# Audio tower on one core: the middle stage rebuilt around four filter buffers, quarter stores and a split triangular solve

## The chip, the cores and the metric

The kernel runs on one core of a Trainium2 chip. The metric is the device time of one execution in microseconds (us), lower is better. Everything is 32-bit float. The engines are named as the profile names them: PE (TensorE, matrix products), PEld (its weight loads), DVE (VectorE), ACT (ScalarE), POOL (GpSimd) and SP (SyncE, which only issues transfers here).

## The reference, cut to what matters

The input is `x`, 32 batches of 750 tokens by 256 features. Tokens are padded to 768, cut into segments of 256 and every second one is kept, so 384 tokens per batch remain, in three blocks of 128.

1. `h = softmax(x x^T / 16) x` inside each block.
2. `h += attn(layernorm(h))`: q, k and v projections with a causal convolution of 4 taps and SiLU; a delta rule in chunks (of 32 in the reference, 128 in the kernel); a short (3 taps) and a long (63 taps) causal filter over v; a gate of two layers over the features and the means and deviations of the four branches; a softmax over the branches; a mixture, a norm and the output projection.
3. `h += ffn(layernorm(h))`: a router picks 2 of 6 experts; each expert is 256 -> 128 -> 256 with GELU.

The delta rule needs, for each chunk, the inverse of `I + A` with `A` strictly lower triangular:

```python
A = jnp.tril(jnp.einsum('bhnid,bhnjd->bhnij', kbc, kc), -1)
T = jnp.linalg.inv(jnp.eye(chunk, dtype=q.dtype) + A)
fir_long = causal_dwconv(vf, fir_long_w.reshape(NH * DV, FIR_L))   # 63 taps per channel
```

## The kernel before, in words

Each engine runs a queue of its own, written out by hand in program order; they meet only through semaphores. A `Signal` is a semaphore with so many increments per iteration; `now(it)` waits for this iteration's, `before(it, back)` for an earlier one's. There are three stages, separated by blocks: no engine enters the next block until all have left the one before.

**First stage** (`first_phase`): block attention, projections, convolutions, the products for `A`. It writes per batch the packs `packa` (q, k, v and scales), `packb` (residual, normed input, short filter) and the 32 x 32 `systems` (1,536 of them: 32 batches x 12 head-blocks x 4) to DRAM, keeps v of all batches in `v_all` (128 partitions x 256 channels x 96 columns), and expands the filter taps to the matrices `toeplitz` in DRAM.

**Middle stage** (`second_phase`), which the change rebuilds:

- PE (L909, L913) runs 32 iterations of 8 channels. Each has two halves of 4 channels; a half is 4 products of a 128 x 128 filter matrix with 96 columns of `v_all` and 4 of a 128 x 62 one with 64 columns. The profile counts each product as two matmuls, so 8 of each per half. The matrices come through two buffers `toep` that SP loads (L896), 760 KB per iteration.
- ACT (L926) copies each half out of PSUM into `stage`, 384 columns. After half of the channels it stores them to DRAM as `fl` in three pieces of 2 MB, one before each further part of its loop; the other half of the channels is written over the part of `v_all` that was read, and stored in three pieces after the last copy (L931). ACT leaves the block when all six have landed.
- DVE inverts the systems by columns: 12 per partition in four groups of three, each group a memset of the diagonal (L965) and 30 columns of two operations, a product (L970) and a sum (L974). POOL loads a group (L951) and stores it when solved (L954). Group g holds every partition's systems 3g to 3g+2, which are a quarter of the systems of every batch.

Then come, one after another with all engines in step: `prime`, a block in which SP increments the third stage's signals; and a block in which SP loads that stage's weights (L832), the first packs (L1111, L1117), the filtered values (L1114), the residual (L1120) and the solved systems into `UF` (L1108), while ACT and DVE compute a few constants and DVE clears `UF`, `TL`, `S`, `SGT` and part of `w1s` (L1142 to L1175). SP loads `UF` only after DVE's clears.

**Third stage** (`third_phase`): a software pipeline of bodies, one per batch, in which batch n is in the delta rule, `it = n-1` in the gate and the mixture, `e = n-2` in the router and the first experts, and `f = n-3` in the last experts. On DVE a body is, in this order: masks of the products (`mask`, L1653), `branch_statistics`, `transpose_diagonal` (L1659), `add_expert(f, 3)`, `residual(e)`, `add_expert(f, 4)`, `input_stats(n)` (L1664; it waits for the loads of pb and fl), `second_norm(e)` (L1775), `gate_logits(it)` (L1711, waits for PE's L1361), `add_expert(f, 5)`, `gate_weights`, `weigh`, `state(n, 0)` (L1685), the router, and the remaining additions (L1740, L1826). On PE the gate's products (L1350, L1354, L1361) stand between the merges of the inverse (L1254 to L1284, which read `UF` and `TL`) and `updates(n, 0)` (L1313). SP's body stores the result, loads the next packs each after the wait for its buffer's last reader, and then `load_u(n + 2)`. DVE writes out the first four bodies and loops over the others two by two.

Of the kernel before, what the change touches and what calls it, by code (L numbers as in the profile page):

```python
# [10 lines left out]
P = 128  # L11
D = 256
# [15 lines left out]

QT, KBT, KT, KTOK, VTOK = (n * HALF * T for n in range(5))
# [22 lines left out]

def even_heads_first(blk, h):

    return (h % 2) * (NM // 2) + blk * (NH // 2) + h // 2


def audio_tower(nc, x, w, out):
    NB = x.shape[0]
    NSYS = NB * NM * NQ // P  # L60
    with ExitStack() as ctx:
# [8 lines left out]
        def signal(name, per=1, primed=1):  # L70
# [7 lines left out]
            "fl": nc.dram_tensor("fl", [NB, P, BLK * D], F32, kind="Internal").ap(),  # L78
# [12 lines left out]
        shared = dict(expanded=expanded, NB=NB, NSYS=NSYS, dram=dram, bank=bank, ident=ident, upper=upper)  # L91
        make_constants(nc, ctx, ident, upper)
        with nc.sbuf_tensor("v_all", [P, D, BLK * NB], F32) as v_all:
            first_phase(nc, x, w, shared, v_all)
            second_phase(nc, shared, v_all)
        third_phase(nc, w, out, shared, third_phase_weights(nc, ctx))


# [709 lines left out]
def third_phase_weights(nc, ctx):  # L808
    def sb(name, shape):
# [15 lines left out]
    loaded = ctx.enter_context(nc.semaphore("p3_weights"))  # L825
    return dict(w1g=w1g, w1s=w1s, b1g=b1g, w2g=w2g, b2g=b2g, wo=wo, onw=onw, router=router, anchors=anchors,
                rclip=rclip, w1e=w1e, w2e=w2e, itemp=itemp, loaded=loaded)


def load_third_phase_weights(nc, sp, w, tail):  # L830
    def load(dst, src):
        sp.dma_start(dst, src).then_inc(tail["loaded"], 16)  # L832

    load(tail["w1g"][:, :, :], w["mlp_w1"][0:D].rearrange("(a p) n -> p a n", a=HALF))
    load(tail["w1s"][0:GATE_S, :], w["mlp_w1"][D:])
    load(tail["w2g"][:, :, :], w["mlp_w2"].rearrange("(m p) n -> p m n", m=MC))
    load(tail["wo"][:, :, :], w["Wo"].rearrange("(a p) n -> p a n", a=HALF))
    for e in range(NE):
        load(tail["w1e"][:, :, e, :], w["ffn_w1"][e].rearrange("(a p) n -> p a n", a=HALF))
    load(tail["w2e"][:, :, :], w["ffn_w2"].rearrange("e p n -> p e n"))  # L840
    load(tail["b2g"][:, :], w["mlp_b2"].partition_broadcast(P))
    load(tail["anchors"][:, :, :].rearrange("p e d -> p (e d)"), w["ffn_anchors"].rearrange("e d -> (e d)").partition_broadcast(P))
    load(tail["rclip"][:, :], w["ffn_routing_temp"].partition_broadcast(P))
    load(tail["itemp"][:, :], w["gate_log_temp"].partition_broadcast(P))
    for half in range(2):
        load(tail["onw"][half * DH:(half + 1) * DH, :], w["o_norm_w"].unsqueeze(1))
    with nc.allow_non_contiguous_dma(reason="a few columns, once"):
        load(tail["b1g"][:, :], w["mlp_b1"].rearrange("(m p) -> p m", m=MC))
        for a in range(HALF):
            load(tail["router"][:, a, :], w["ffn_proj_w"][:, a * P:(a + 1) * P].rearrange("e p -> p e"))  # L850


def second_phase(nc, shared, v_all):


    NB, NSYS, dram, bank, expanded = (shared[k] for k in ("NB", "NSYS", "dram", "bank", "expanded"))
    CG = 8
    SG = 3
    with ExitStack() as c:
# [9 lines left out]
        toep = [sb(f"toep{s}", [P, CG, TW]) for s in range(2)]  # L869
        Xs = [sb(f"X{s}", [P, SG, SC, SC]) for s in range(2)]  # L870
        GC = D // 2
        GI = GC // CG

        stage = [sb("stage", [P, BLK * NB, GC]),
# [13 lines left out]
        with nc.Block() as block:  # L888
# [30 lines left out]
            def _(act):  # L919
# [16 lines left out]
                for b in range(BLK):  # L936
                    store(0, b)
                    copy_pairs(1, b * 2, b * 2 + 2 if b < BLK - 1 else GI // 2)
                act.wait_ge(*fl_copied.now(2 * GI - 1))
                for b in range(BLK):  # L940
                    store(1, b)
# [1032 lines left out]
```

## Time and profile before

| | us |
|---|---|
| median of 3 runs (2932.5 to 2945.92) | 2935.69 |
| the profiled execution, its own time | 2936.39 |
| its span in the trace | 2934.7 |
| PE busy in the span | 2552.5 (87%) |
| DVE busy in the span | 1916.4 (65%) |
| ACT busy in the span | 1371.2 (47%) |
| POOL busy in the span | 532.7 (18%) |
| mean granted TensorE clock, share of full speed | 0.888 |

The profile cuts the span into 40 equal slices of 73.4 us and gives the busy tenths of each engine in each. `PEclk` is the granted TensorE clock in tenths of full speed; 0.50 is 1.2 GHz and 1.00 is 2.4 GHz. The first stage ends in the 11th slice, the middle stage fills slices 11 to 14. Elsewhere, rows have a start, a duration, the engine, the line of the kernel, the operation with its output and input, shapes and count, and in square brackets how long the engine had been idle and who ended that.

### The profile page before, as it was taken

What the parts mean: (1) busy time and instruction counts of PE and PEld (TensorE: products, weight loads), DVE (VectorE), ACT (ScalarE), POOL (GpSimd) and SP (SyncE); (2) the same over time, 40 slices, a digit from 0 to 9 for tenths busy, and PEclk for the clock granted to TensorE, in tenths of its full rate; (3) what the DMA queues carried; (4) which work ended last, traced back from release to release, by engine and by line L of the source; (5) the groups of instructions that cost most, each with busy time, mean ns of one, the idle gap of its engine ahead of it and who ended that gap; (6) DMA issues with size and microseconds to landing.
All of it is one profiled execution on the core that took longest, in us unless ns stands there. A gap on an engine that the chain in (4) does not pass through costs nothing.

```text
span 2934.7 us, 60213 instructions
## 1 busy us (share of the span) xinstructions
PE 2552.5 (87%) x21024; PEld 1936.5 (66%) x21024; DVE 1916.4 (65%) x5240; ACT 1371.2 (47%) x2626; POOL 532.7 (18%) x375
## 2 busy tenths in 40 slices
PE   5888888888699279999999999999999999999997
PEld 3666666666588257767676766766766677667765
DVE  4888898888599024655665765566566647655664
ACT  3777777777222123443444434434534444344442
POOL 1333333333100001111111111111111111111110
PEclk9999999999655557998999999999999999999998
DMA  2566566666567612212211311221122113111200
GB/s 73 197 215 205 190 214 202 200 205 207 194 213 235 192 68 95 66 58 87 81 63 58 108 59 64 66 100 65 58 91 77 63 58 107 60 64 63 101 17 16
DMA packets 233222, 334.12 MB, mean 114 GB/s; under 512 B 113696, under 2 KB 198656, under 8 KB 223776
## 3 DMA queue, kind: packets, MB, share of 16 engines
q1 hardware_dynamic: 207168, 305.89, 31.6%
q10 hardware_dynamic: 24672, 12.58, 1.5%
q0 software_dynamic: 1152, 12.58, 1.1%
q8 instruction: 144, 2.36, 0.3%
q14 instruction: 86, 0.70, 0.1%
HBM read 191.68 MB, written 164.23 MB: 121 GB/s over the span
## 4 chain that ended last, share of the span: by engine, by line
PE 42%; DVE 11%; ACT 6%; issue 6%; DVEq 0%; ACTq 0%; POOL 0%
PE bank L1407 6%; PE bank L1417 6%; PE bank L1350 5%; PE bank L1361 3%; PE bank L1379 3%; PE bank L1245 3%; PE bank L1328 3%; ACT L1554 3%; PE bank L1354 2%; PE bank L1313 2%; PE bank L1276 2%; PE bank L1284 2%; DVE DL L1740 1%; DVE HA L1826 1%; DVE bst L1762 1%
## 5 line engine op out<-in xcount | busy, mean ns | idle before, releaser
L1407 PE MATMUL bank<-YT,w1e 128*128 128x384 f32 x768 | 321.1, 545 | 1.2 <-ACT HE L1554 1.2
L683 DVE SCALAR_TENSOR_TENSOR Y<-bank,convw,Y 128x383 f32<-128x383 f32 (+2 forms) x576 | 315.2, 607 | 6.0 <-ACT Y L559 6.0
L1417 PE MATMUL bank<-w2e,HE 128*128 128x256 f32 x1152 | 308.9, 407 | 10.8 <-DVE HA L1826 7.8
L1826 DVE SCALAR_TENSOR_TENSOR HA<-bank,we,HA 128x256 f32<-128x256 f32 x576 | 242.8, 476 | 112.5 <-PE bank L1417 108.7
L411 PE MATMUL bank<-pb,wqkv 128*128 128x384 f32 x768 | 286.4, 503 | 10.4 <-DVE pb L667 9.5
L1711 DVE TENSOR_TENSOR L<-bank,b2g 128x48 f32<-128x48 f32 x32 | 6.6, 208 | 420.2 <-PE bank L1361 420.2
L1417 PEld LDWEIGHTS bank<-w2e,HE 128*128 128x128 f32 x1152 | 219.0, 201 | 51.6 <-issue 14.7
L1554 ACT ACTIVATE HE<-bank 128x384 f32<-128x384 f32 x192 | 94.3, 491 | 232.7 <-PE bank L1407 232.0
L1350 PE MATMUL bank<-qb,w1g 128*128 128x384 f32 x512 | 201.8, 517 | 0.4 <-ACT GH L1546 0.4
L1407 PEld LDWEIGHTS bank<-YT,w1e 128*128 128x128 f32 x768 | 150.5, 214 | 75.5 <-issue 27.8
L1245 PE MATMUL bank<-qa 64*128 64x256 f32 x768 | 118.9, 431 | 92.2 <-PEq L1123 57.9
L1537 ACT ACTIVATE ATM<-bank 128x192 f32<-128x192 f32 x192 | 60.2, 331 | 296.0 <-DVE ATM L1653 296.0
L411 PEld LDWEIGHTS bank<-pb,wqkv 128*128 128x128 f32 x768 | 138.4, 197 | 84.3 <-issue 14.7
L783 POOL TENSOR_TENSOR RR<-RS,minus_half 128x24 f32<-128x24 f32 x32 | 133.3, 4166 | 272.0 <-DVE RS L732 272.0
L1929 POOL TENSOR_TENSOR ta<-qb,WT 128x768 f32<-128x768 f32 x32 | 72.6, 2267 | 542.7 <-DVE WT L1730 542.7
L1245 PEld LDWEIGHTS bank<-qa 64*128 64x128 f32 x768 | 71.5, 199 | 139.6 <-issue 125.9
L559 ACT ACTIVATE Y<-bank,convw 128x384 f32<-128x384 f32 x192 | 112.2, 584 | 79.9 <-PE bank L411 78.8
L909 PE MATMUL bank<-v_all,toep 128*128 x512 | 129.5, 434 | 20.6 <-DMA toep<-toeplitz 17.5
L1935 POOL TENSOR_TENSOR m<-m,minus_half_q 128x12 f32<-128x12 f32 x32 | 72.6, 2270 | 372.9 <-DVE m L1746 372.9
L909 PEld LDWEIGHTS bank<-v_all,toep 128*128 128x128 f32 x512 | 114.0, 328 | 28.3 <-issue 21.6
L1328 PEld LDWEIGHTS bank<-W,ATM 128*128 128x128 f32 x768 | 108.0, 212 | 35.8 <-ACT W L1529 25.7
L1328 PE MATMUL bank<-W,ATM 128*128 128x64 f32 x768 | 114.5, 298 | 15.0 <-ACT W L1529 15.0
(220 smaller groups left out, 5459.2 us busy)
## 6 DMA issues: line engine op xcount, KB each, us to landing
packa<-pa SPq DMA_DIRECT2D x32, 1932.0 KB, 6.3
qa<-packa SPq DMA_DIRECT2D x32, 1932.0 KB, 7.7
packb<-pb SPq DMA_DIRECT2D x32, 768.0 KB, 5.1
qb<-packb SPq DMA_DIRECT2D x32, 768.0 KB, 6.7
toeplitz<-taps SPq DMA_DIRECT2D x128, 190.0 KB, 4.4
toep<-toeplitz SPq DMA_DIRECT2D x32, 760.0 KB, 4.2
packb<-fsk SPq DMA_DIRECT2D x32, 384.0 KB, 2.3
fl<-fl SPq DMA_DIRECT2D x32, 384.0 KB, 5.4
```

What stands on the lines that cost most here:

```text
L411: mm = pe.matmul(proj_bank[j][:, 0:T], wqkv[:, a, j * P:(j + 1) * P], xnT[:, a, :], start=(a == 0), stop=(a == HALF - 1))
L559: act.activation(Y[:, j, :], proj_bank[j][:, 0:T], ACT.Copy, scale=convw[:, j, CK - 1:CK])\
L683: dve.scalar_tensor_tensor(out=Y[:, j, lag:T], in0=proj_bank[j][:, 0:T - lag], scalar=convw[:, j, CK - 1 - lag:CK - lag], in1=Y[:, j, lag: ...
L783: pool.tensor_tensor(RR[:, :, :, :].rearrange("p b n h -> p (b n h)"), RS[:, :], minus_half[:, :], ALU.pow)\
L909: pe.matmul(acc[:, o:o + BLK * NB], toep[s][:, ch, 0:P], v_all[:, it * CG + ch, :], start=(k == 0), stop=False, skip_group_check=True)
L1245: mm = pe.matmul(bank[odd][:, hh * 2 * P:(hh + 1) * 2 * P], kT[rows, hh, pair * P:(pair + 1) * P], qkb[rows, :, hh, pair * P:(pair + 1) * ...
L1328: mm = pe.matmul(bank[1][:, h * DH:(h + 1) * DH], ATM[:, even_heads_first(b, h), 0:P], W[:, h, :], start=(b == 0 and h == 0), stop=True, s ...
L1350: pe.matmul(mlp_bank[m][:, 0:T], w1g[:, a, m * P:(m + 1) * P], chans(pb[s], PX)[:, a, :], start=(a == 0), stop=False)
L1407: mm = pe.matmul(bank[6][:, 0:T], w1e[:, a, k, :], YT[s][:, a, :], start=(a == 0), stop=(a == HALF - 1))
L1417: mm = pe.matmul(expert_bank(b), HE[k % 2][:, b * P:(b + 1) * P], w2e[:, k, :], start=True, stop=True)
L1554: act.activation(HE[k % 2][:, :], bank[6][:, 0:T], ACT.Gelu_apprx_tanh).then_inc(he_ready.sem, 1)
L1826: dve.scalar_tensor_tensor(out=HA[s][:, b, :], in0=expert_bank(b), scalar=we[s][:, b, k:k + 1], in1=HA[s][:, b, :], op0=ALU.mult, op1=ALU. ...
```

## The change

All of it is in the middle stage, in the block that stood behind it, and in what the third stage had to take over:

- `toep` has four buffers instead of two; SP's loop is written out.
- Channels go in four groups of 64. Each group's filtered values are laid out as `fl` wants them, [head][partition][batch, block, channel], and stored in four quarters of 768 KB, each one contiguous run of 6 KB per partition. Group g's quarters are issued while group g+1 is copied, the last one behind that group's last copy; those of the last group after the end. The third stage reads `fl` in rows of 768 bytes instead of 3,072. ACT no longer waits for the stores inside the block; SP does so at the head of the third stage, before it loads the packs of batch 1 and `fl`.
- The third stage's buffers lie in the memory of `v_all` and of the first group, so its clears and loads can be made as soon as the region is free. The clears move from DVE to ACT (`between`), the constants into gaps of the middle stage, the weights to SP's queue behind toep 5 to 20, the signals' priming to SP behind toep 4, the packs of batch 0 behind toep 26 (after a wait for the stores of group 1), `load_u` of batches 0 and 1 to the end of SP's queue.
- A solve group is now a quarter of the batches (0 to 7, 8 to 15, ...). DVE solves groups 0 and 1 and columns 1 to 19 of group 2 in the middle stage. Columns 20 to 30 of group 2 stand in the third stage's DVE bodies 0 to 5 (3, 3, 2, 1, 1, 1 of them), all 30 of group 3 in bodies 6 to 20, two in each, between `second_norm` and `gate_logits`. For this DVE's bodies 0 to 21 are written out and only the rest is a loop. SP stores group 2 after its body 9 and group 3 after its body 21, and waits for those before bodies 14 and 22.
- The block of loads and clears and the separate `prime` are gone.

```diff
-        toep = [sb(f"toep{s}", [P, CG, TW]) for s in range(2)]
+        toep = [sb(f"toep{s}", [P, CG, TW]) for s in range(NT)]        # NT = 4
@@ SP, middle stage
-                with sp.Fori(0, D // CG // 2) as i:
...
+                for it in range(groups):
+                    if it >= NT:
+                        sp.wait_ge(*fl_ready.now(it - NT))
+                    sp.dma_start(toep[it % NT][:, :, :], dram["toeplitz"][:, it * CG:(it + 1) * CG, :])\
+                        .then_inc(toep_loaded[it % NT].sem, 16)
+                    if it == NT:
+                        for g in tail["signals"]:
+                            sp.sem_inc(g.sem, g.per * g.primed)
+                    if it > NT:
+                        load_third_phase_weight(nc, sp, w, tail, it - NT - 1)
+                    if it == groups - 6:
+                        load_packs(sp)
+                load_factors(sp, setup_act)
+                sp.wait_ge(loaded, 16 * WEIGHT_LOADS)
@@ ACT, middle stage
+                def store(g, q):
+                    part = NB * BLK * DH // FQ
+                    act.dma_start(dram["fl"][g][:, q * part:(q + 1) * part], stage[g][:, q * part:(q + 1) * part])\
+                        .then_inc(tail["fl_stored"][g], 16)
...
+                    if g == 2 and j == 3:
+                        act.wait_ge(loaded, 16 * WEIGHT_LOADS)
+                        clear(tail["w1s"][SC:2 * SC, :], slice(SC, 2 * SC), MLP)
...
+                    if g == 2 and j == 4:
+                        act.wait_ge(tail["fl_stored"][0], 16 * FQ)
+                        clear(tail["UF"][0], slice(0, P), NM * P)
...
+                for g in range(NH):
+                    for j in range(GI):
+                        copy_group(g, j)
+                        if g and j % 2:
+                            if j == 1:
+                                act.wait_ge(*fl_copied.now(g * GI - 1))
+                            store(g - 1, j // 2)
+                        between(g, j)
+                act.wait_ge(*fl_copied.now(NH * GI - 1))
+                for q in range(FQ):
+                    store(NH - 1, q)
+                act.wait_ge(setup_act, CLEARED)
@@ DVE, middle stage
+                solve["begin"](dve, 0)
+                for j in range(1, SC - 1):
+                    solve["column"](dve, 0, j)
...
+                solve["begin"](dve, 2)
+                for j in range(1, SPLIT):                                # SPLIT = 20
+                    solve["column"](dve, 2, j)
@@ SP, helpers and third stage
+        def load_packs(sp):
+            sp.wait_ge(fl_stored[1], 16 * FQ)
+            load_a(sp, 0, 0)
+            load_b(sp, 0, 0)
+        def load_factors(sp, setup_act):
+            sp.wait_ge(setup_act, CLEARED)
+            sp.wait_ge(solve_stored, 16)
+            load_u(sp, 0, 0)
+            load_u(sp, 1, 1)
...
+                sp.wait_ge(fl_stored[2], 16 * FQ)
+                load_a(sp, 1, 1)
+                load_b(sp, 1, 1)
+                sp.wait_ge(fl_stored[3], 16 * FQ)
+                load_fl(sp, 0, 0)
+                load_fl(sp, 1, 1)
+                load_h(sp, 0)
...
+                sp.wait_ge(solve_stored, 16 * 2)
+                bodies(4, 10)
+                store_solved(2)
+                bodies(10, 14)
+                sp.wait_ge(late_stored, 16)
+                bodies(14, 22)
+                store_solved(3)
+                sp.wait_ge(late_stored, 16 * 2)
+                bodies(22, NB - 2)
@@ DVE, third stage
+                    if columns is not None:
+                        g, first, last = columns
+                        if first == 1:
+                            solve_begin(dve, g)
+                        for j in range(first, last):
+                            solve_column(dve, g, j)
                     if have_it:
                         gate_logits(it)
...
+                for n in range(3, 21):
+                    body(n, n - 1, n - 2, n - 3, 1 - n % 2, n // 2, columns_of(n))
+                body(21, 20, 19, 18, 0, 10)
+                with dve.Fori(9, NB // 2 - 2) as i:
```

## Rows read from the trace of the kernel before

**Rows 1.** The page's slices: busy tenths of PE, granted clock, GB/s.

```profile
span 2934.7 us, 60213 instructions
PE   5888888888699279999999999999999999999997
PEclk9999999999655557998999999999999999999998
```

**Rows 2.** Stretches: length, busy time of each engine, granted clock, DMA share, GB/s.

```profile
774.90:973.96 199.06, 192.07 (x1024) 173.37 (x1024) 163.17 (x244) 53.68 (x64) 3.23 (x6) 0.50 0.63 212
973.96:1030.90 56.94, 0.00 (x0) 0.00 (x0) 6.34 (x21) 1.90 (x5) 0.05 (x1) 0.50 0.77 219
780.00:870.00 90.00, 90.00 (x483) 81.42 (x484) 85.01 (x132) 25.16 (x30) 1.61 (x3) 0.50 0.54 184
```

**Rows 3.** Middle stage in order of time: one half of an iteration, and the last.

```profile
867.74 2.02 PE L909 MATMUL bank<-v_all,toep 128*128 x8
...
869.69 1.11 PE L913 MATMUL bank<-v_all,toep 128*62 x8
...
870.73 2.02 PE L909 MATMUL bank<-v_all,toep 128*128 x8
...
971.91 1.11 PE L913 MATMUL bank<-v_all,toep 128*62 x8
973.15 0.81 ACT L926 ACTIVATE v_all<-bank 128x384 f32 x1 [2.15 <-PE bank L913]
973.99 13.13 ACTq L931 DMA_DIRECT2D fl<-v_all  x3
1002.31 0.39 SPq L832 DMA_DIRECT2D w1g<-in_L_attn_mlp_w_dram  x1
```

**Rows 4.** Waits from 755 to 1060 us: total, times, longest.

```profile
PE bank L909 <- DMA toep<-toeplitz: 17.5, 3, 14.5
PE bank L909 <- ACT v_all L926: 3.1, 3, 1.0
```

**Rows 5.** Windows of 2 us and 10 us behind the last copy, columns as rows 2.

```profile
994.00:996.00 2.00, 0.00 (x0) 0.00 (x0) 0.00 (x0) 0.00 (x0) 0.00 (x0) 0.50 1.00 290
1032.00:1034.00 2.00, 1.02 (x6) 0.30 (x2) 0.95 (x3) 0.52 (x2) 0.32 (x1) 0.50 1.08 443
```

**Rows 6.** DVE, the last solve group, in order of time.

```profile
909.28 0.14 DVE L965 MEMSET X<- 128x96 f32 x1 [0.16 <-DVE X L974]
...
928.86 0.91 DVE L970 TENSOR_TENSOR prod<-X 128x720 f32<-128x720 f32 x1
...
932.63 0.90 DVE L970 TENSOR_TENSOR prod<-X 128x714 f32<-128x714 f32 x1
...
938.17 0.84 DVE L970 TENSOR_TENSOR prod<-X 128x660 f32<-128x660 f32 x1
...
943.25 0.73 DVE L970 TENSOR_TENSOR prod<-X 128x552 f32<-128x552 f32 x1
...
951.81 0.33 DVE L974 TENSOR_TENSOR X<-X,prod 128x90 f32<-128x90 f32 x1
```

**Rows 7.** Head of the third stage in order of time.

```profile
1029.83 0.46 SPq L1120 DMA_DIRECT2D hf<-packb  x1
1030.94 2.08 PE L1245 MATMUL bank<-qa 64*128 64x256 f32 x8 [57.92 <-PEq L1123]
1040.25 0.29 DVE L1664 BATCH_NORM_STATS2 ST<-qb 128x6 f32<-128x128 f32 x1
1043.57 0.28 DVE L1664 BATCH_NORM_STATS2 ST<-qa 128x6 f32<-128x128 f32 x1
1057.86 0.59 DVE L1685 COPY S<-bank 64x128 f32<-64x128 f32 x2 [14.01 <-PE bank L1321]
```

**Rows 8.** DMA issues by line: count, KB each, median us to landing.

```profile
toep<-toeplitz SPq DMA_DIRECT2D x32, 760.0 KB, 4.2
qa<-packa SPq DMA_DIRECT2D x32, 1932.0 KB, 7.7
qb<-packb SPq DMA_DIRECT2D x32, 768.0 KB, 6.7
fl<-fl SPq DMA_DIRECT2D x32, 384.0 KB, 5.4
```

**Rows 9.** DVE's waits from 1208 to 2800 us, as rows 4.

```profile
DVE L L1711 <- PE bank L1361: 363.5, 28, 13.0
```

**Rows 10.** Third stage: the same four products before and after the clock rose.

```profile
1086.05 2.93 PE L1350 MATMUL bank<-qb,w1g 128*128 128x384 f32 x4
1091.09 1.56 PE L1350 MATMUL bank<-qb,w1g 128*128 128x384 f32 x4
```

More of the change, by code:

```diff
@@ L840, in load_third_phase_weights @@
[L840 to L856, printed above, removed]
+    if n == 0:
+        sp.dma_start(tail["itemp"][:, :], w["gate_log_temp"].partition_broadcast(P)).then_inc(tail["temp_loaded"], 16)
+        sp.dma_start(tail["rclip"][:, :], w["ffn_routing_temp"].partition_broadcast(P)).then_inc(tail["temp_loaded"], 16)
@@ L930, in store @@
-                def store(g, b):
-                    act.dma_start(dram["fl"][:, :, b * D + g * GC:b * D + (g + 1) * GC].rearrange("n p c -> p n c"),
-                                  stage[g][:, b * NB:(b + 1) * NB, :]).then_inc(fl_stored, 16)
-                copy_pairs(0, 0, GI // 2)
-                act.wait_ge(*fl_copied.now(GI - 1))
[L936 to L939, printed above, removed]
@@ L940, in _, with copy_group @@
-                for b in range(BLK):
-                    store(1, b)
-                act.wait_ge(fl_stored, 16 * BLK * 2)
+                def copy_group(g, j):
+                    it = g * GI + j
+                    out = stage[g].rearrange("p (n b c) -> p c b n", n=NB, b=BLK)
+                    for half in range(2):
+                        act.wait_ge(*fl_ready.now(it, half + 1))
+                        act.activation(out[:, j * CG + half * 4:j * CG + half * 4 + 4],
+                                       bank[2 * (it % 2) + half][:, 0:4 * BLK * NB].rearrange("p (c b n) -> p c b n", c=4, b=BLK),
+                                       ACT.Copy).then_inc(fl_copied.sem, 1)
@@ L955, in _ @@
-                pool.wait_ge(sys_stored, 16 * groups)
+                X = solve["X"]
+                for g in range(NG - 1):
+                    pool.dma_start(X[g][:, :, :, :], systems[g]).then_inc(solve["loaded"][g], 16)
+                for g in range(NG - 2):
+                    pool.wait_ge(solve["step"], (g + 1) * SOLVE_STEPS)
+                    pool.dma_start(systems[g], X[g][:, :, :, :]).then_inc(solve["stored"], 16)
+                    pool.wait_ge(solve["stored"], 16 * (g + 1))
@@ new lines, in third_phase @@
+        second_phase(nc, w, shared, v_all, stage, tail,
+                     dict(X=X, step=solve_step, loaded=solve_loaded, stored=solve_stored, begin=solve_begin, column=solve_column),
+                     load_packs, load_factors)
+        hf = sb("hf", [P, HALF * T])
+        P1 = sb("P1", [P, NM, SC])
+        P1B = sb("P1B", [P, NM, DH])
+        VB = sb("VB", [P, NM, DH])
+        R = sb("R", [P, NH, DH])
+        W = sb("W", [P, NH, DH])
+        DL = [sb(f"DL{s}", [P, NM, DH]) for s in range(2)]
@@ L1178, in third_phase @@
+        me, se, re = (sb(f"g{n}", [P, BLK]) for n in range(3))
         with nc.Block() as block:
```

385 lines of the change are left out of this document (205 added, 180 removed).

## The prediction, as it was made before the result was known

> **What bounds the kernel now.** I first read the busy tenths and the clock per slice. PE is at 8 or 9 tenths nearly everywhere; the deepest notch is slice 14 (954 to 1,027 us) with 2 tenths, and around it the granted clock stays at 5 tenths for four slices [rows 1]. So two things are special in the middle: an idle stretch, and a slow clock. The windows cut them apart. From 774.90 to 973.96 us PE is busy 192.07 of 199.06 us at clock 0.50; from there to 1030.90 us PE does nothing at all for 56.94 us [rows 2]. Behind that comes the third stage, 1,904 us long (2934.7 - 1030.9), which the change touches only with small additions.
>
> Inside the middle stage one half-iteration takes 870.73 - 867.74 = 2.99 us [rows 3], and there are 64: 191.4 us of PE work back to back. The stretch from PE's first matmul at 774.9 to its last end at 971.91 + 1.11 = 973.0 is 198.1 us, so about 6.7 us are stalls. The waits name them: PE waited 17.5 us for filter loads, of which 14.5 was the wait before the start, and 3.1 us for ACT's copies [rows 4]: 6.1 us inside. DVE is busy 163.17 us of the same stretch [rows 2], its last column ends at 952.1 [rows 6], 21 us before PE. So in the middle PE at 1.2 GHz is the bound and DVE is not.
>
> The idle 57.9 us (973.0 to 1030.94) is a chain of things in sequence: ACT's last copy, 6.3 MB of stores after it, the priming, then from 1002.31 weights, constants, clears, packs, factors [rows 3, 7]. None of it needs to be behind PE's last product, except the last stores and what reads them.
>
> **The middle stage, PE.** The matmuls are the same, so 191.4 us at this clock. Four buffers can take back at most the 6.1 us; stores of one contiguous run per partition, spread over the stage, should disturb loads less than the bursts of 2 MB. Against it: the stage's traffic grows by three loads moved into it (weights, packs, factors), and at the start four filter loads and three solve groups are issued together instead of two and two. The tightest place is behind toep 26: SP waits there for the last store of filter group 1, which ACT issues behind its copy of iteration 23. With an iteration of 5.98 us, SP is free about 149 us into PE's work (24 iterations, 144 us, the copy, and about 4.5 us for a store, as toep's 4.2 us for the same size [rows 8]); it then issues 2,700 KB of packs before toep 27, which PE needs at 27 x 5.98 = 161.5. Packs and toep 27, 3.5 MB, take 8 us at 443 GB/s and 12.2 at 290 [rows 5], with about 2 of latency (an estimate, from 4.2 us for 760 KB against 443 GB/s), landing at 160 to 164: a stall of 0 to 3 us. I take 2 us of stalls in all and 1 us for a later start: 191.4 + 3 against 198.1, a gain of 3.7 us. Bounds: a gain of 7 (no stall), and a loss of 10, if PE waits at the pack loads, the weight loads and the start as long as a landing of qb (6.7 us [rows 8]) each.
>
> SP's priming (some 90 increments) lies behind toep 4, with three filters in stock. ACT's clears are priced by its 384-column copy, 0.81 us [rows 3]: 5,504 columns in all, 11.6 us at that rate, in five iterations in which ACT has 5.98 - 1.7 us each to spare; PE's two-iteration lead covers them. ACT's wait for the weights (iteration 19's copy) comes three iterations after their last load is issued, 18 us against landings of 5.4 to 7.7 us [rows 8]. I cost these at nothing; the range bounds them.
>
> **DVE in the middle.** One group takes 952.1 - 909.3 = 42.9 us [rows 6]. Two groups and columns 1 to 19 (938.17 - 909.28 = 28.9) are 114.7 us, about 12 more waiting for the weights: DVE ends near 912. It was not the bound at 952 and is not now, so what leaves it earns nothing here; it only lets the batch-wise factors be stored early. What leaves has to be paid or hidden later.
>
> **The gap.** Behind PE's last product stand the last copy (0.96 us to its end), four issues at about 0.4 us (the pieces that did not queue took 0.38 to 0.44), and the change of block, 0.65 us from 1030.29 to 1030.94 [rows 7]: 3.2 us; I take 4. PE's first product of batch 0 needs only pa 0, loaded before. So 57.9 becomes 4: a gain of 53.9 us. If the issues queue as the 13.13 us of three did before [rows 3], it is 14 and the gain 44: those were rows of 512 bytes, twelve times as many pieces as four quarters of 6 KB.
>
> **Body 0, what is late next.** DVE's statistics wait for fl 0, which waits for the last quarters. After the end five quarters are out (one of group 2, four of group 3), 3.9 MB, and 2.8 MB of packs for batch 1 are issued beside them. 6.7 MB take 15 us at 443 GB/s and 23 us at 290 [rows 5]; I take 17 to the landing of the last store, since it need not wait for all packs, and 5.4 for fl 0 [rows 8]: 22.4 us after PE's end, 18.4 after the third stage starts. Behind the waiting statistics are queued 3.6 us of themselves (1040.25 to 1043.85) and now three columns, 943.25 - 938.17 = 5.1 us [rows 6]. DVE is free at 27.1; PE has the first state ready at 1057.86 - 1030.94 = 26.9 us [rows 7]. So nearly even: 0 at the fast rate, 8 us late at the slow one. I take +2 us.
>
> By the Trainium skill ("DMA: Bandwidth & Descriptors", section "Bandwidth") transfers should be batched to 1 MiB or more for three quarters of a peak of about 425 GB/s; the quarters of 768 KB lie under that, which speaks against cutting them. By that rule they still run near 320 GB/s and the term stays under 6 us; the trace shows 2 MB pieces at 290 GB/s with all DMA engines busy [rows 5], so size alone did not give them the peak.
>
> **Columns in the third stage.** Columns 20 to 30 are 952.1 - 938.2 = 13.9 us, group 3 is 42.9: 56.8 us of DVE work, at most 932.63 - 928.86 = 3.8 us in a body from 6 on. They stand exactly where DVE waits for PE's gate: 363.5 us in 28 bodies, 13.0 each [rows 9]. Behind the columns on DVE stands `gate_logits`, and PE's outputs wait for it later; it still has 9 us in hand. Bodies 1 to 5 have 4.3 us or less (six operations of 0.73 us and below) under the same cover. If the cover were gone, 56.8 us would be lost; I take 1 us. The two waits of SP for stored groups (1.5 MB) stand before a wait for `h2_ready` of the same body: nothing. fl in rows of 768 bytes: the load has a body of time. Nothing.
>
> **Sum.** -3.7 - 53.9 + 2 + 1 = -54.6 us from the profiled execution's 2936.4: 2881.8. That execution was 0.7 us over the median, so I predict 2881.
>
> **Rivals.** A, the clock rises in the middle stage. The Trainium skill ("TensorE: Matmul & The Clock Gate", Part 1) says that a throttled array is released by sustained activity. This trace speaks against it here: 90.00 of 90.00 us busy, and 0.50 throughout [rows 2]. What a full clock gives is shown by the gate's products, 2.93 us against 1.56 [rows 10], so 191 us would be 102; DVE's 115 to 127 us and the traffic then bind: toep 24.9 MB, three quarters of fl 9.4, solve groups 9.4, weights and packs about 5, 49 MB at a mean of 330 GB/s (between the rates of [rows 5]), 148 us against 194. Time 2881 - 46 = 2835. Against it: the matmuls and the idle stretch before them are unchanged. 7%.
>
> B, the columns are not hidden: a body's DVE chain turns out to be the bound, and 56.8 us come back: about 2937. The 13.0 us of waiting per body speak against it [rows 9]. 6%.
>
> C, the end of the stage stays serial in part: stores and packs at 290 GB/s or slower, SP in its fixed order, DVE's body 0 late by 15 to 20 us. Time about 2898. For it: everything hangs on the last store, and the loads of pa 1 and pb 1 go ahead of fl. 11%.
>
> D, the other sign: DVE's bodies 3 to 20 written out. In place of a loop DVE runs 18 bodies of code used once. If its instructions arrive late, every such body is longer outside the cover; to be slower by 0.5% this must cost (54.6 + 14.7) / 18 = 3.9 us per body. At 4.5 us it gives 2881 + 81 = 2962. Against it: the first bodies before were written out too, and DVE started the third stage's first operations without such a wait [rows 7]. 5%.
>
> **How the numbers follow.** The forecast has 67%, C 11, A 7, B 6, D 5, 4 for mixtures. About 0.5%, 14.7 us, is what a measurement of this kernel can tell from no change, so faster means under 2921: forecast, C, A and half of the mixtures, 0.87. Same 0.06 (B). Slower 0.07 (D and the rest). The forecast's own bounds are 2881 - 7 and 2881 + 13 + 8; with C the range is 2863 to 2905.
>
> **What would show it.** Right: the stretch of `toep` products at 194 +- 3 us with clock 0.50; 3 to 5 us between the last of them and PE's first product of batch 0; DVE's copy of the first state 26.9 to 32 us after that product; DVE's wait at `gate_logits` down from 13.0 to about 9.3 us in bodies 6 to 20, and unchanged in 22 to 31; a body as long as before. Wrong: a clock above 0.5 in the middle (A), PE waiting for DVE in bodies with columns and not in those without (B), DVE idle for issue in the written-out bodies (D), PE idle over 10 us in body 0 (C).

## The result, and the profile after

| | median us (range, runs) | ratio to before, 95% interval | profiled span, clock |
|---|---|---|---|
| before | 2936.5 (2932.5 to 2945.9, 4) | 1 | 2934.7, 0.888 |
| after | 2836.9 (2831.6 to 2847.3, 4) | 0.966 [0.963, 0.970] | 2845.5, 0.896 |

The change gives 99.6 us by the medians; 54.6 were forecast, and 2836.9 lies below the range of 2863 to 2905. The profiled execution of after is the slowest of its four (2847.3), so the two traces differ by 89.2 us, and the ledger below is made against that.

First the windows that answer to [rows 2] (length, busy time of PE, PEld, DVE, ACT, POOL, granted clock, DMA share, GB/s), from PE's first filter product to its last end, from there to batch 0, and the 90 us of before:

```profile
772.60:964.30 191.70, 191.69 (x1024) 173.33 (x1024) 110.32 (x168) 59.40 (x74) 1.61 (x3) 0.50 0.68 247
964.30:969.81 5.51, 0.00 (x1) 0.03 (x1) 0.00 (x0) 0.81 (x1) 0.10 (x1) 0.50 0.87 353
780.00:870.00 90.00, 90.00 (x482) 81.43 (x482) 81.06 (x123) 25.41 (x32) 0.54 (x1) 0.50 0.66 230
```

The middle stretch fell from 198.1 to 191.7 us and has no stall left; the gap fell from 57.9 to 5.5; the clock stayed at its lower level (0.50 of 2.4 GHz). The end of the middle stage in order of time, all engines, answers to [rows 3, 7]:

```profile
963.18 1.11 PE L952 MATMUL bank<-v_all,toep 128*62 x8
964.33 0.81 ACT L964 ACTIVATE v_all<-bank 128x384 f32<-128x384 f32 x1 [2.17 <-PE bank L952]
964.33 4.83 ACTq L970 DMA_DIRECT2D fl<-v_all  x5
969.61 0.35 SPq L1193 DMA_DIRECT2D v_all<-packa  x1
969.81 2.08 PE L1348 MATMUL bank<-v_all 64*128 64x256 f32 x8 [5.52 <-PEq L918]
...
984.59 0.30 DVE L1767 BATCH_NORM_STATS2 ST<-v_all 128x6 f32<-128x128 f32 x1 [5.39 <-DMA first_stage<-fl]
...
996.72 0.59 DVE L1792 COPY first_stage<-bank 64x128 f32<-64x128 f32 x2 [3.57 <-PE bank L1424]
```

The first product of batch 0 follows 5.5 us behind. ACT's first issue (0.34 us) runs beside the last copy; the four behind the copy fill 3.99 us (965.17 to 969.16), and three of these took 1.05, 1.23 and 1.29 us. DVE waits 5.4 us for the first filtered batch, but copies the first state at 996.72, which is 26.9 us after that product, as before ([rows 7]: 1057.86 - 1030.94), and it waits there for PE. Body 0 lost nothing.

DVE's waits at `gate_logits` (L1818) in bodies 6 to 20, with two columns each (1310 to 2150 us), and in those behind, without columns (2150 to 2740), total, times, longest, against [rows 9]:

```profile
DVE L L1818 <- PE bank L1464: 136.9, 15, 10.4
...
DVE L L1818 <- PE bank L1464: 142.9, 11, 13.0
```

9.1 us each with columns, 13.0 without: the columns lie in waits, as forecast (9.3 and 13.0).

Ledger of the two profiled executions: start of the middle stage -2.3, middle stretch -6.4, gap -52.4, together -61.1; and the last stage, from PE's first product of batch 0 to the end, 1903.8 to 1875.7, -28.1. That last term was forecast at +3. PE's waits in 30 bodies, first of before (1104.28 to 2822.62 us), then of after (1043.18 to 2730.90):

```profile
PE bank L1245 <- issue: 28.3, 13, 2.5
PE bank L1313 <- DVE R L1676: 23.1, 22, 1.2
PE bank L1338 <- ACT ATM L1537: 22.1, 29, 2.8
```

```profile
PE bank L1416 <- DVE R L1783: 23.0, 22, 1.2
PE bank L1348 <- issue: 19.1, 6, 3.7
PE bank L1441 <- ACT v_all L1640: 13.7, 29, 2.8
```

L1245 (after: L1348) is the first product of a body. Its wait "issue", for nothing the profile shows, stood at every one of the 13 back edges of PE's loop (the jumps from its end to its start), which has two bodies a pass; after, at 6 of 13. I call such a wait a stall. The wait for ACT's mask copies fell by 8.4. And the same 12,254 matmuls took less time:

```profile
1104.28:2822.62 1718.34, 1593.99 (x12254) 1198.44 (x12254) 1034.57 (x3084) 734.33 (x1338) 250.19 (x150) 0.94 0.22 73
```

```profile
1043.18:2730.90 1687.72, 1581.38 (x12254) 1190.03 (x12253) 1097.35 (x3155) 733.53 (x1338) 253.86 (x150) 0.95 0.23 76
```

Of the 30.6 us, 18.0 are waiting and 12.6 are shorter busy time of the same products, at a mean clock of 0.95 instead of 0.94. The part behind these bodies is 2.5 us longer, which leaves the 28.1. What removed the waits was the question for the runs.

### The profile page after: what moved, and what is told of

It reads as the page before. It is cut to its first block, busy times and chain, and to the rows that moved or that the text cites. A ratio compares the mean times of both kernels' runs of the same rounds, so it can differ in the third digit from the quotient of the medians.

```text
span 2845.5 us, 59121 instructions
## 1 busy us (share of the span) xinstructions
PE 2540.7 (89%) x21024; PEld 1928.7 (68%) x21024; DVE 1929.1 (68%) x5233; ACT 1374.4 (48%) x2633; POOL 535.0 (19%) x373
## 4 chain that ended last, share of the span: by engine, by line
PE 45%; DVE 10%; ACT 6%; issue 4%; DVEq 0%; ACTq 0%
PE bank L1510 7%; PE bank L1520 7%; PE bank L1453 5%; PE bank L1348 4%; PE bank L1464 3%; PE bank L1482 3%; PE bank L1431 3%; ACT L1657 3%; PE bank L1457 2%; PE bank L1416 2%; PE bank L1379 2%; PE bank L1387 2%; DVE DL L1852 2%; DVE v_all L1938 1%; PE bank L1473 1%
## 5 line engine op out<-in xcount | busy, mean ns | idle before, releaser
L1510 PE MATMUL bank<-v_all,w1e 128*128 128x384 f32 x768 | 318.9, 542 | 1.3 <-ACT HE L1657 1.3
L1938 DVE SCALAR_TENSOR_TENSOR v_all<-bank,we,v_all 128x256 f32<-128x256 f32 x576 | 242.8, 477 | 99.6 <-PE bank L1520 97.4
L1818 DVE TENSOR_TENSOR L<-bank,b2g 128x48 f32<-128x48 f32 x32 | 6.7, 208 | 349.1 <-PE bank L1464 349.1
L1453 PE MATMUL bank<-v_all,w1g 128*128 128x384 f32 x512 | 201.8, 517 | 0.4 <-ACT v_all L1649 0.4
L1510 PEld LDWEIGHTS bank<-v_all,w1e 128*128 128x128 f32 x768 | 149.0, 212 | 74.9 <-issue 26.2
L1640 ACT ACTIVATE v_all<-bank 128x192 f32<-128x192 f32 x192 | 60.1, 331 | 269.3 <-DVE v_all L1756 269.3
L2057 POOL TENSOR_TENSOR v_all<-v_all,WT 128x768 f32<-128x768 f32 x32 | 72.5, 2267 | 529.5 <-DVE WT L1837 529.5
L1348 PE MATMUL bank<-v_all 64*128 64x256 f32 x768 | 118.9, 432 | 30.6 <-issue 19.1
L1632 ACT ACTIVATE first_stage<-bank 32x384 f32<-32x384 f32 (+1 forms) x192 | 89.0, 479 | 106.7 <-PE bank L1368 43.2
L1756 DVE TENSOR_TENSOR v_all<-bank,upper 128x256 f32<-128x256 f32 x192 | 72.2, 418 | 93.0 <-PE bank L1348 92.2
L1431 PEld LDWEIGHTS bank<-W,v_all 128*128 128x128 f32 x768 | 108.2, 213 | 36.0 <-ACT W L1632 25.7
L948 PEld LDWEIGHTS bank<-v_all,toep 128*128 128x128 f32 x512 | 114.0, 328 | 20.9 <-issue 13.7
```

What stands on the lines that cost most here:

```text
L948: pe.matmul(acc[:, o:o + BLK * NB], toep[s][:, ch, 0:P], v_all[:, it * CG + ch, :], start=(k == 0), stop=False, skip_group_check=True)
L1348: mm = pe.matmul(bank[odd][:, hh * 2 * P:(hh + 1) * 2 * P], kT[rows, hh, pair * P:(pair + 1) * P], qkb[rows, :, hh, pair * P:(pair + 1) * ...
L1431: mm = pe.matmul(bank[1][:, h * DH:(h + 1) * DH], ATM[:, even_heads_first(b, h), 0:P], W[:, h, :], start=(b == 0 and h == 0), stop=True, s ...
L1453: pe.matmul(mlp_bank[m][:, 0:T], w1g[:, a, m * P:(m + 1) * P], chans(pb[s], PX)[:, a, :], start=(a == 0), stop=False)
L1510: mm = pe.matmul(bank[6][:, 0:T], w1e[:, a, k, :], YT[s][:, a, :], start=(a == 0), stop=(a == HALF - 1))
L1938: dve.scalar_tensor_tensor(out=HA[s][:, b, :], in0=expert_bank(b), scalar=we[s][:, b, k:k + 1], in1=HA[s][:, b, :], op0=ALU.mult, op1=ALU. ...
```

## The experiments

The measure beside the time is L, the length from PE's first product of body 2 to that of body 31, read from each profiled execution (before 2790.67 - 1124.01 = 1666.7). It leaves the middle stage and the first bodies out. "Waits" is the part of L in which PE was not busy. The stalls are those with the cause "issue" in L, at the first product of a body on PE and at the first mask of a body on DVE. The packets are those of the queues q8 and q14 from 1200 to 2600 us; what they are is told under e4. Ratios are to before on the same chip. A difference between two kernels is given by the medians and, where it matters, also by the ratios, since the experiments ran on more than one chip.

| kernel | median | ratio [95%] | L | waits | PE, DVE stalls | q8, q14 packets |
|---|---|---|---|---|---|---|
| before | 2936-2944 | 1 | 1666.7 | 120.4 | 13, 0 | 107, 60 |
| after | 2836.9 | 0.966 [0.963, 0.970] | 1636.1 | 102.4 | 6, 0 | 56, 22 |
| e1_dve_loop | 2873.7 | 0.977 [0.974, 0.979] | 1664.7 | 108.1 | 5, 8 | 49, 62 |
| e2_before_dve_out | 2914.0 | 0.991 [0.987, 0.994] | 1650.7 | 112.9 | 13, 0 | 108, 33 |
| e3_before_pe_shift | 2940.2 | 1.001 [0.999, 1.002] | 1667.7 | 115.7 | 3, 10 | 26, 60 |
| e4_before_pe_hint | 2916.6 | 0.993 [0.991, 0.995] | 1644.8 | 113.2 | 0, 13 | 7, 62 |
| f1_after_pe_hint | 2818.5 | 0.959 [0.957, 0.961] | 1612.5 | 83.3 | 0, 0 | 4, 22 |
| f2_after_all_hints | 2823.7 | 0.962 [0.960, 0.964] | 1614.1 | 82.6 | 0, 0 | 4, 21 |
| f3_dve_loop_hint | 2846.9 | 0.969 [0.967, 0.971] | 1634.9 | 95.4 | 3, 0 | 31, 3 |
| f4_after_pe_place | 2852.7 | 0.973 [0.970, 0.976] | 1644.2 | 107.5 | 13, 0 | 110, 22 |
| g1_before_both | 2886.8 | 0.981 [0.979, 0.984] | 1617.7 | 87.5 | 0, 4 | 7, 36 |
| m1_two_buffers | 2847.7 | 0.968 [0.965, 0.970] | 1620.9 | 79.9 | 0, 0 | 5, 22 |
| m2_late_packs | 2833.8 | 0.963 [0.960, 0.966] | 1615.7 | 80.9 | 0, 0 | 6, 22 |
| h1_dve_no_loop | 2825.5 | 0.960 [0.957, 0.962] | 1616.8 | 78.9 | 0, 0 | 4, 27 |

The rest of L is the busy time of the same products. It still differs by up to 27 us (1529.2 in f1, 1556.6 in e1), at a mean granted clock of 0.95 or 0.94, and not in the order of the waits. One profiled execution of each kernel therefore says more about waits than about L.

### Which edit made the last stage shorter

**e1_dve_loop**: after, with VectorE's loop as it was. It also leaves out the columns of the last stage, so the rest of group 2 and group 3 stay unsolved, and the stores and waits of SP that went with them.

```
@@ SP and DVE, the columns and their stores left out
...
@@ DVE
-                for n in range(3, 21):
-                    body(n, n - 1, n - 2, n - 3, 1 - n % 2, n // 2, columns_of(n))
-                body(21, 20, 19, 18, 0, 10)
-                with dve.Fori(9, NB // 2 - 2) as i:
+                body(n=3, it=2, e=1, f=0, s=0, npair=1)
+                with dve.Fori(0, NB // 2 - 2) as i:
```

> The changed kernel, but VectorE runs its bodies from 4 on as a loop of two bodies, as the kernel before does, and the columns of the last stage are left out (the rest of group 2 and group 3 of the systems stay unsolved), with one loop of SyncE. In the trace of after the columns lie in waits (VectorE's wait at gate_logits fell from 13.0 to 8.2-11.2 in the bodies that had them), so leaving them out gives nothing by any theory. Theory 1 (PE's stalls at its loop's back edge, 13 of 13 before and 6 of 13 after, some 3.5-4 us each, became fewer because VectorE no longer goes round a loop of its own at the same time): the stalls are back at 13 of 13 and the time is 2837 + 7 x 3.7 = 2863, range 2855-2875. Theory 2 (the stalls became fewer because the code ahead of PE's loop is 132 instructions longer, so that the loop lies elsewhere): as after, 2832-2842, 5-7 stalls. Theory 3 (the 28 us came from where the data lies, the loads or the first bodies): also as after, but with the stalls not deciding.

Measured +36.8 us against after (+31 by the ratios). L is back at 1664.7, near that of before. So the unforecast gain hangs on how VectorE's bodies are written, and with a loop there the rest of the change, new layouts and buffers included, left the length of the bodies as it was. But PE had only 5 stalls, not 13: theory 1 had the edit right and its mechanism wrong. Of the 28.5 us that L is over that of after, only 5.7 are waits of PE; 22.8 are longer products. The mean granted clock over the whole execution was 0.889 to 0.896 in the four runs of e1 and 0.896 to 0.901 in those of after, so this is no accident of one trace; what lowers the clock is not shown.

**e2_before_dve_out**: before, with VectorE's bodies 4 to 21 written out.

```
-                with dve.Fori(0, NB // 2 - 2) as i:
+                for n in range(4, 22):
+                    body(n, n - 1, n - 2, n - 3, 1 - n % 2, n // 2)
+                with dve.Fori(9, NB // 2 - 2) as i:
```

> The kernel before, with VectorE's bodies 4 to 21 written out and its loop from body 22 on; nothing else changed. Theory 1 (VectorE's loop makes PE's stalls at its back edge): 13 stalls become about 6 and the time falls by 7 x 3.7 = 26, to 2905-2918. Theories 2 and 3: no change, 2933-2940, 13 stalls. If written-out code starved VectorE instead, it would be slower than 2940.

-24.3 us, inside the forecast of theory 1, but with all 13 stalls of PE in place (27.5 us). What fell among the waits is PE's wait for ACT's copies of the masks, 22.1 to 13.7 us; about as much again (8.5 us of L) is shorter products.

**e3_before_pe_shift**: before, with more code ahead of PE's last loop.

```
-                with pe.Fori(0, D // CG // 2) as i:
-                    for s in range(2):
-                        it = i * 2 + s
-                        pe.wait_ge(*toep_loaded[s].now(i))
+                with pe.Fori(0, D // CG // 4) as i:
+                    for four in range(4):
+                        it, s = i * 4 + four, four % 2
+                        pe.wait_ge(*toep_loaded[s].now(i * 2 + four // 2))
```

> The kernel before, with TensorE's loop of the middle stage written with four groups of channels per pass instead of two, as in after: the same products in the same order, and 132 more instructions ahead of TensorE's loop of the last stage. Theory 2 (the place of that loop in the code decides): stalls fall from 13 to about 6, time 2905-2918. Theories 1 and 3: no change in the last stage; the middle stage can gain or lose up to 2 us by half as many back edges: 2931-2939, 13 stalls.

Theory 2 had the stalls right (3 are left) and the time wrong: nothing was won. In the passes where PE no longer stalls, it waits for ACT instead, 14.2 us in 10 places, just behind. Something on another engine is as late as PE was: DVE now has 10 stalls of its own.

**e4_before_pe_hint**: before, with a prefetch hint for the taken branch of PE's loop.

```
-                with pe.Fori(0, NB // 2 - 2) as i:
+                with nc.Fori(0, NB // 2 - 2, engines=[pe.engine], hint_back_edge=True) as i:
```

> The kernel before, with a prefetch hint for the back edge of TensorE's loop of the last stage. If the 2-us waits at the first product of each second body are a fetch of instructions after a taken branch (common to theories 1 and 2), the hint takes the 13 of them away and the time falls by 13 x 3.5 to 4 = 45-52, to 2884-2892. If these waits are something else that the profile calls by no name (the register arithmetic of the loop, a data wait that it misses), nothing changes: 2933-2940.

All 13 stalls went, but only 21.6 us. The start of a pass in before, in order of time, PE and then DVE:

```profile
1343.31 1.51 PE L1417 MATMUL bank<-w2e,HE 128*128 128x256 f32 x6
1346.94 1.13 PE L1245 MATMUL bank<-qa 64*128 64x256 f32 x8 [2.11 <-issue]
...
1350.10 1.13 PE L1245 MATMUL bank<-qa 64*128 64x256 f32 x8
```

```profile
1348.49 0.75 DVE L1653 TENSOR_TENSOR ATM<-bank,upper 128x256 f32<-128x256 f32 x2 [2.27 <-PE bank L1245]
```

and in e4, the same operations:

```profile
1346.46 1.13 PE L1245 MATMUL bank<-qa 64*128 64x256 f32 x8
...
1351.09 1.13 PE L1245 MATMUL bank<-qa 64*128 64x256 f32 x8 [1.40 <-ACT ATM L1537]
```

```profile
1346.65 1.27 DVE L1826 SCALAR_TENSOR_TENSOR HA<-bank,we,HA 128x256 f32<-128x256 f32 x3 [0.15 <-PE bank L1417]
1349.92 0.76 DVE L1653 TENSOR_TENSOR ATM<-bank,upper 128x256 f32<-128x256 f32 x2 [2.00 <-issue]
```

With PE's stall gone, DVE's first mask is late by a stall of DVE's own, 2.00 us with the cause "issue". In before the profile put DVE's idle time down to PE, because PE's stall fell at the same moment. ACT copies behind the mask, and PE's second products wait 1.40 us for ACT. In before the two stalls covered each other. The other runs bear this out. DVE's stalls at its first mask, from the waits of e1, e3 and e4:

```profile
DVE v_all L1749 <- issue: 15.8, 8, 2.1
```

```profile
DVE ATM L1653 <- issue: 20.2, 10, 2.2
```

```profile
DVE ATM L1653 <- issue: 26.3, 13, 2.2
```

With PE's 5, 3 and 0 stalls each makes 13: at every back edge exactly one of the two shows. The instruction queues say which engine is which (1200 to 2600 us, packets, MB, share), before, e4, and then f3, in which DVE's loop has the hint:

```profile
q8 instruction: 107, 1.75, 0.5%
q14 instruction: 60, 0.49, 0.1%
```

```profile
q14 instruction: 62, 0.51, 0.1%
q8 instruction: 7, 0.11, 0.0%
```

```profile
q8 instruction: 31, 0.51, 0.2%
q14 instruction: 3, 0.02, 0.0%
```

A hint on PE's loop empties q8, and one on DVE's empties q14, which had 62 packets in e1, the same kernel without it. Across the runs q8 goes with PE's stalls: 107 to 110 packets with 13 stalls, 56 with 6, 49 with 5, 26 and 31 with 3, 4 to 7 with none. So the loop's code was fetched again at the back edges that stalled, in before at all 13. The hint does not only fetch earlier, since the packets go too; how it does that is not shown. The Trainium skill ("Runtime: NRT & Kernel Launch", section "Instruction fetch mechanics") says that branching breaks the sequential prefetch and that a taken branch can wait for a fetch of its target. The 13 stalls of 2.2 us and their end by the hint agree.

### The revised theory, tested

Theory 1': each engine stalls about 2 us at its own back edge, DVE's being hidden behind PE's in before.

**f1_after_pe_hint**: after, with the one-line edit of e4.

> The changed kernel with a prefetch hint for the back edge of TensorE's loop of the last stage. In the kernel before the same hint took all 13 stalls away and gave 21.6 us, less than 13 x 3.5, because VectorE's own stall of 2.0 us at its first mask of the pass then showed through ScalarE's copies (TensorE's wait for ATM of 1.4 us in 13 passes). Theory 1' (each engine with a loop body longer than its fetch blocks stalls at its own back edge, and the two stalls cover each other, so that one alone gives less than both): in the changed kernel VectorE's is gone in passes 1 to 9, so the 6 stalls of 19.1 us go whole, 6 x 3.7 = 22: 2810-2822. Rival (TensorE's stalls no longer cost anything here, since data waits take their place): 2832-2838.

-18.4 us (-21 by the ratios), inside the forecast; L 1612.5, no stall. The waits fell by 19.1 us, which is the sum of the 6 stalls of after. This kernel beats both. A pass start now:

```profile
1336.16 1.14 PE L1348 MATMUL bank<-v_all 64*128 64x256 f32 x8
...
1339.33 1.13 PE L1348 MATMUL bank<-v_all 64*128 64x256 f32 x8
```

3.17 us from the first products to the second, and no wait before either.

**f3_dve_loop_hint**: e1 with the same hint on VectorE's loop.

> The kernel of the first of these runs (VectorE in a loop from body 4 on, the columns of the last stage left out; 2873.7 against 2836.9), with a prefetch hint at VectorE's back edge. Theory 1' (VectorE's fetch of instructions after its taken branch is what the written-out bodies save): the hint gives the same as writing out, 2832-2842. Rival (the two shapes differ in something else, the columns' timing, SyncE's loops or the place of data): no change, 2868-2880.

-26.8 us against e1 (-22 by the ratios), and L 1634.9 against after's 1636.1. This is the cleanest pair, since the two kernels differ in the hint alone. So it was the fetch, not the shape of the written-out code: a hint on the loop does for the length of the bodies what writing them out did. Of the 29.7 us of L, 12.7 are waits and 17.1 shorter products. The median is 10 us over that of after and above the forecast, against 0.3 us between the two profiled spans; that difference stays open.

**f4_after_pe_place**: after, with PE's loop at before's place in the code.

```
-                with pe.Fori(0, NB // 2 - 2) as i:
+                with nc.Fori(0, NB // 2 - 2, engines=[pe.engine], head_slot={pe.engine: 189}) as i:
```

> The changed kernel, with the head of TensorE's loop of the last stage at the same slot of a fetch block as in the kernel before (189 instead of 65). Theory 2' (the place of TensorE's loop halves its stalls and counts once VectorE's are gone; in the kernel before, with VectorE's in place, it gave nothing): 13 stalls again and +7 x 2 to 3.7 = 14-26 less what their kind costs less: 2845-2862, that is what remains between the 36.8 of writing out here and the 24.3 there. Rival (the place gives nothing here either): 2832-2842.

+15.8 us by the medians (the intervals of the two ratios just touch), 13 stalls, 110 packets on q8. Theory 2' holds: the place of PE's loop counts once VectorE's stall is gone. Its size is less sure: L rose by 8.0 us and the stalls in sum only from 19.1 to 26.2, because the 6 of after are longer (five of 3.2 to 3.7 us) than the 13 here (1.7 to 2.4). That the loop lies elsewhere in after is an accident of the change: its middle loop is longer.

**g1_before_both**: the edits of e2 and e4 together.

> The kernel before, with both single edits at once: VectorE's bodies 4 to 21 written out (alone -24.3 us) and the prefetch hint at the back edge of TensorE's loop of the last stage (alone -21.6 us). Theory 1' (the two stalls fall at the same moment of a pass and cover each other): both together give more than the sum of 45.9; by the clean passes of the changed kernel with the hint (111.4 us a pass against 114.6 before, 14 passes, and 4 of them still with VectorE's stall) 50 to 58: 2878-2887. Rival (the two are independent and add): 2888-2893. If one of them already had the whole of it: 2905-2915.

-57.0 us by the medians, inside the forecast. Ratio 0.981 [0.979, 0.984], where the two single ratios add up to 0.984: the interval does not settle it. The single profiled executions do: L fell by 48.9 together, 16.0 and 21.8 alone, and the waits of PE alone by 32.9 together, 7.5 and 7.2 alone. DVE keeps 4 stalls of 2.0 us in its last passes. L is 1617.7 here and 1612.5 to 1616.8 in f1 and h1: the old kernel's bodies are about as long as the new one's.

**f2_after_all_hints**: after, hints on the loops of TensorE, ScalarE and VectorE in all stages.

> The changed kernel with prefetch hints at the back edges of all loops of TensorE, ScalarE and VectorE in the three stages. Theory 1': beside the 22 of the last stage's loop of TensorE, VectorE's last 4 passes give 4 x 1.5 = 6, and the first stage's 31 waits of 1.17 us at TensorE's back edge (36.4 us in the trace) go as far as they are on the path, between 0 and 36: 2775-2812. Rival (those of the first stage are the loop's own branch or a wait for data under another name): 2805-2815, with the 31 waits still there.

5.2 us above f1, not below, with bodies as in f1 (L 1614.1). The 31 waits of the first stage stayed (36.3 us): the rival was right that these are no fetch at the back edge. Without the hints q8 has 1 packet in 600 us of the first stage (after, 100 to 700 us), so there was next to nothing to take away. What these waits are stays open.

**h1_dve_no_loop**: f1, VectorE's bodies 22 to 31 written out as well.

> The changed kernel with the hint on TensorE's loop (2818.5), with VectorE's bodies 22 to 31 written out too, so that VectorE goes round no loop in the last stage. Theory 1': the last passes still carry VectorE's stall of 2.0 us in four back edges, worth 1.5 to 2.5 each after ScalarE's copies: -6 to -10, 2808-2813. Rival (VectorE's stall in the last passes is covered by something else): 2816-2821.

Nothing was won: ratio 0.960 against 0.959. The forecast stood on a stall that f1 does not have. Its DVE has no wait "issue" at the first mask of any pass, though it goes round its loop in the last ones, and PE waits there for no mask. In g1, whose last passes are a loop as well, the four stalls stand. The instruction queue of DVE in those passes, in f1 (2200 to 2700 us) and in g1 (2260 to 2760), and g1's wait:

```profile
q14 instruction: 1, 0.01, 0.0%
```

```profile
q14 instruction: 21, 0.17, 0.1%
```

```profile
DVE ATM L1653 <- issue: 7.9, 4, 2.0
```

So this run takes no stall away and says nothing on the price of one: PE's waits in L fell by 4.4 us, its products took 8.7 longer. Why the same loop is fetched again in g1 and not in f1 was not tested; its place in the code differs, as with PE's loop in f4.

### Two terms of the middle stage

**m1_two_buffers**: f1 with `NT = 2`.

> The changed kernel with the hint on TensorE's loop (2818.5), with two filter buffers instead of four. The prediction gave four buffers about half of the 6.1 us of waits in the middle stage (3.1 for ScalarE's copies, 3.0 for the transfer of toep). If the buffers took both away: +3 to +6, 2821-2825, with waits for the transfer back in the middle stretch. Rival (the waits were those of the old stores' long issues and of the loads that ran beside them, so two buffers are enough now): 2817-2820, a middle stretch of 192 us as in after.

+29 us by medians (+25 by ratios). PE's waits from 755 to 1000 us:

```profile
PE bank L948 <- DMA toep<-toeplitz: 28.9, 15, 13.5
```

13.5 is the start, so 15.4 us of waits for filters are in the stretch, against none with four buffers. PE reached batch 0 at 986.82 instead of 969.68, 17.1 us later. The bodies behind it were longer by 8 us (L 1621) although their waits were 3.4 us shorter: their products ran at a granted clock of 0.92 against 0.97 in 1100 to 1300 us. That this comes of the buffers is not shown. In the middle stage four buffers let the early weights, packs and stores ride beside the filters.

**m2_late_packs**: f1 with `load_packs` at the head of the last stage.

> The changed kernel with the hint on TensorE's loop (2818.5), with the packs of batch 0 loaded at the head of the last stage instead of beside the middle one. By the prediction the landing of packa then stands between the middle and the last stage: its issue at the stage's start and 7.6-7.7 us to land, so the first product of batch 0 comes 13 us after the last product of the middle stage instead of 5.5, +7 to +9: 2826-2828. Rival (the first product waits no longer than now, because something else ends last there): 2818-2821.

+15.2 by medians, +12 by ratios. PE's first product of batch 0, and from the view of DMA issues the landing of the packs (count, KB each, us):

```profile
979.76 2.08 PE L1348 MATMUL bank<-v_all 64*128 64x256 f32 x8 [16.96 <-DMA v_all<-packa]
```

```profile
v_all<-packa SPq DMA_DIRECT2D x2, 1932.0 KB, 14.0
```

The kind of wait is as forecast, its size was not: behind the last quarters, with four packs at once, a pack lands in 14.0 us, not in the 7.7 of a quiet moment [rows 8].

## Why the prediction was wrong

**The step that failed** is the third stage, "which the change touches only with small additions", and "a body as long as before". It was put at +3 us and measured -28.1 in the profiled executions; taking VectorE's written-out bodies out again (e1) gives back 36.8 by the medians, 31 by the ratios. The bodies are shorter because VectorE no longer waits about 2 us for its code at the head of each pass (e2, f3), and because PE's loop came to lie where it stalls in 6 passes of 13 instead of in all (f4: 15.8 us by the medians, 8.0 in L). These figures come from different kernels and do not add up to the 28.1. The waits are traced to the fetch; the other part of the gain, the shorter products at a slightly higher clock (12.6 of 30.6 us), came with these edits, but how it follows from them stays open.

What I did with the written-out bodies was rival D: a loss, if instructions come late. I bounded that edit on one side. The row that speaks for a gain was there and not read: PE's 28.3 us of "issue" in 13 places, one per pass. DVE's own stall could not be read among the waits of before, since it stood under PE's name; only the 60 packets on q14 pointed at it.

**Without that step** the sum is near. Up to batch 0 it had -57.6 and the traces show -61.1. e1 is the change without it (and without the columns): 2873.7 by the median, inside the range but 7 us under the 2881; the profiled spans differ by 56.6 us, the medians by 64.5. The measured 2836.9 lies next to rival A's 2835, which is a coincidence: A's clock did not come. And the low end of the range, 2863, does not follow from the bounds given, of which the lower is 2874.

- The middle stretch: 191.7 measured, with no stalls where I kept 2 us, and a start 2.3 us earlier where I had 1 us later. Rightly a small term, yet m1 shows that "at most 6.1 us" was the worth of four buffers in the old surroundings; in the new ones it is 15.4 of waits for filters, 17.1 us at batch 0 and about 25 in time.
- The gap: 57.9 to 4 forecast, to 5.5 measured. The four issues behind the last copy took 3.99 us where I took four at 0.4 us: three of them took over 1 us each, a milder form of the 13.13 us for three in [rows 3].
- Body 0: +2 forecast, 0 measured. DVE waited for fl, but the first state came at 26.9 us as before.
- Columns: +1 forecast, hidden. The wait at `gate_logits` fell to 9.1 on average in bodies 6 to 20, and to 8.2 in the body with the shortest, 9.3 forecast.
- Rival A (clock): 0.50 in 90.00 of 90.00 busy us, as before. The trace of after gives the rule of the Trainium skill ("TensorE: Matmul & The Clock Gate", Part 1), that sustained activity releases a throttled array, no more support here than that of before. B and C did not come: there was a gain in the bodies with columns, and PE waited nowhere over 10 us in body 0. D came with the other sign.

## What to carry to other kernels

Read a wait called "issue" that stands once per pass of a loop as a price of the loop, and expect an engine that idles at the same moment to have one of its own under the other's name: fix both, since one alone may give little or nothing. Before a loop is written out for another reason, put a price with both signs on it, and try a hint at the back edge, which costs one line. A buffer's worth is measured among the transfers that the change brings, not among those of before.

## What the runs showed of the hardware

- Where a back edge of a long loop stalled, PE stood 1.7 to 3.8 us and DVE 2.0 to 2.2 us; with the hint, q8 fell from 107 packets to 4 to 7 in 1,400 us, so nearly nothing of PE's loop was fetched again, which I had not expected of a body this long.
- Where PE stalled at a back edge, DVE's stall lay under it and bore PE's name; it showed as "issue" only in the passes in which PE did not stall (8 in e1, 10 in e3, 13 in e4).
- Moving PE's loop in the code changed the count of stalls from 13 to 3 (e3) and 6 (after), and moving it back restored 13 (f4).
- The same products took 1529.2 to 1556.6 us of busy time in L, at a mean granted clock of 0.95 and 0.94. Fewer waits often went with shorter products (12.6 of the 30.6 us in 30 bodies), but not always: e1 has 12.3 us less of waits than before and 10.3 us more of products.
